# Placing the routing steps of a two-layer transformer kernel earlier and later in its table of steps

## The chip, the core and the metric

The kernel runs on one core of a Trainium2 chip. The metric is the device time of one execution in microseconds (us). A core has five engines, each of which runs its own instructions strictly in order: TensorE (PE, matrix products; its weight loads are listed apart as PEld), VectorE (DVE), ScalarE (ACT), GpSimd (POOL) and SyncE (SP, which here only starts DMA transfers). They wait for each other through semaphores. The before kernel was timed three times: 1833.56, 1834.5 and 1831.23 us, median 1833.56 us.

## What is computed

8192 tokens of width 128 (32 sequences of 256) pass two layers. Layer 0 is a linear attention with 16 heads and rotary positions, beside a mixture of 64 experts of width 64 plus a shared expert. Layer 1 is an attention that keeps the 8 best keys of a row, with a message network over 4 neighbours, followed by a mixture of 8 experts of width 256 of which each token takes 2. Cut to what matters here:

```python
# layer 0, routing: sigmoid scores, 4 of 8 groups, then 8 of 64 experts
scores = sigmoid(x @ router_w.T)
...
coef = zeros((T, E)).at[arange(T)[:, None], topk_idx].add(topk_w)
h = silu(g) * u * coef[:, :, None]
# layer 1, routing: softmax over 8 experts, the best 2
probs = softmax(x @ gate_w.T)
weights, idx = top_k(probs, 2)
weights = weights / sum(weights)
```

Layer 0 computes all 64 experts for every token (the coefficient is zero for the ones not chosen). Layer 1 computes only the two chosen experts of each token: the normalised rows are sent by indirect DMA to slots in HBM that are sorted by expert, and a second phase reads them back block by block.

## The kernel before

Tokens are worked in 16 chunks of 512. In the first phase a chunk is 33 tiles of the layer-0 mixture (32 pairs of experts and the shared expert). One tile is one step `g`; `j` is its number within the chunk, 0 to 32. A step on TensorE is three matmuls into `ps_gate` (L601 to L603), three into `ps_up`, and the down product of three steps earlier into `ps_y` (L656). ScalarE takes `silu` of `ps_gate` (L1260), VectorE multiplies by `ps_up` (L854, `times_up`) and then, a step later, by the coefficients (L848, `times_coef`). The first gate matmul of step g waits for the silu of step g-2, the first up matmul of step g waits for `times_up` of step g-2. So VectorE and ScalarE may be behind by a step and a part, no more.

Everything else (the attention of both layers, the normalisation, the routing of both layers) is cut into small named parts and laid beside those tiles. Tables at the head of the file say at which step `j` a part is put on every engine: `ROUTE0` for the layer-0 routing of the next chunk, `ROUTE1` for the layer-1 routing of the chunk before. An entry of `ROUTE1` at 33 or more falls into the chunk after, at `j` less 33. `make_plan` turns the tables into one list a step, and each engine runs the parts of step `j` that concern it, in the order of the list, behind its tile work:

```python
steps += [(ROUTE1 if c < SPARSE else ROUTE1_LAST, c - 1), (ATTENTION1, c - 1)] if c > 0 else [(PREP1, 0)]
plan[g] += [(what, c - 2) for at, what in ROUTE1 if at == j + TILES0 and c > 1]
plan[g] += [(what, key) for table, key in steps for at, what in table if at == j]
```

The parts of layer-1 routing that carry into the chunk after stand first in the list of their step. They are:

- `rank` (TensorE, L764 and L765): two small products that count the earlier tokens of each expert. It waits for `prefix` on GpSimd.
- `key`, `first2`, `slot` (VectorE; L1065 to L1072, L1076 to L1082, L1085 to L1091): the slot number and the weight of each token. `first2` of a chunk writes `slot_of` (L1082) and waits first until all sends of the chunk before have landed.
- `send0` to `send7` (GpSimd, L1496 to L1503): eight indirect DMAs of 128 rows. Each waits until TensorE has done the gate product of its step; `send0` and `send4` first write two columns of the rows.

The parts of layer-0 routing that the change touches are `sigmoid0` (VectorE: add one, L885, and the reciprocal of one half, L888) and `sigmoid1` (the reciprocal of the other half, L891).

The last chunk of the first phase, number 15, uses the table `ROUTE1_LAST` for chunk 14: `rank` at 17, `first2` at 19, `slot` and `table` (a block table for the second phase, L1171 to L1196) at 20, the sends at 21 to 24. In the same chunk the carried parts of chunk 13 still follow `ROUTE1`. Chunk 0 and chunk 1 have no carried parts.

Three banks of PSUM (`ps_side`) serve all small products in rotation. `make_plan` gives each product a bank when its step is reached and frees it at the step of its reader; TensorE waits for the reader of the bank's last use. Other parts met below: `kv0` to `kv3` (steps 0 to 3: VectorE L971 and L975, then a ScalarE copy L1334), `norm0` (ScalarE L1277, step 2), `q` (TensorE, step 5), `k_rope` (GpSimd L1446, step 4), `q_feat` (GpSimd L1461, step 13), `s0_mask` and `s1_mask` (VectorE L1114, steps 13 and 14), `k_feat` (VectorE L988), `strike0` and `strike1` (VectorE L1129, steps 16 and 17), `attend_exp` (ScalarE L1371, step 18).

Of the kernel before, what the change touches and what calls it, by code (L numbers as in the profile page):

```python
# [70 lines left out]
              (12, "feat_exp"), (13, "q_feat"), (14, "k_feat"), (16, "kvsum"), (17, "kvmask"), (19, "num0"), (20, "num1"), (20, "mix0"),  # L71
              (24, "mix1"), (26, "mixT")]
FINISH0 = [(3, "yT"), (4, "y_add")]
ROUTE0 = [(0, "stats0"), (2, "norm0"), (4, "xT0"), (5, "x_lo0"), (8, "logit0"), (10, "score_exp"), (12, "sigmoid0"), (14, "sigmoid1"),
          (18, "choice"), (18, "pair4"), (19, "pair2"), (20, "pair1"), (21, "gtop"), (22, "gstrike"), (23, "groups"), (24, "top8"),
          (25, "strike"), (26, "weigh"), (28, "coefT")]
ROUTE1 = [(5, "stats1"), (7, "norm1"), (8, "xT1"), (9, "x_lo1"), (10, "vl0"), (10, "vl1"), (11, "top1"), (12, "gate_exp"), (23, "softmax"), (30, "select"),
          (31, "prefix"), (39, "rank"), (40, "key"), (41, "first2"), (42, "slot"), (43, "send0"), (45, "send1"), (47, "send2"), (48, "send3"),
          (49, "send4"), (51, "send5"), (53, "send6"), (54, "send7")]

ROUTE1_LAST = [(5, "stats1"), (7, "norm1"), (8, "xT1"), (9, "x_lo1"), (10, "vl0"), (10, "vl1"), (11, "top1"), (12, "gate_exp"), (14, "softmax"), (15, "select"),
               (16, "prefix"), (17, "rank"), (18, "key"), (19, "first2"), (20, "slot"), (20, "table"), (21, "send0"), (21, "send1"), (22, "send2"), (22, "send3"),
# [25 lines left out]
def make_plan():  # L108
# [11 lines left out]
    for g in range(TILES):  # L120
# [5 lines left out]
        steps += [(ATTENTION0 if c > 0 else EARLY0, c)]  # L126
        steps += [(ROUTE0, c + 1)] if c + 1 < CHUNKS else []
        steps += [(ROUTE1 if c < SPARSE else ROUTE1_LAST, c - 1), (ATTENTION1, c - 1)] if c > 0 else [(PREP1, 0)]
# [1487 lines left out]
```

## Time and profile before

| | us | share of the span |
|---|---|---|
| median of three runs | 1833.56 | |
| the profiled execution's own time | 1833.56 | |
| its span, first to last instruction | 1831.3 | |
| TensorE busy | 1736.6 | 95% |
| VectorE busy | 1348.7 | 74% |
| ScalarE busy | 803.2 | 44% |
| GpSimd busy | 609.8 | 33% |

The span is what the trace shows; 2.3 us of the execution lie outside it. In the chain of work that ended last, 88% is TensorE. Busy time of TensorE is modelled from its pipelined matmuls, so it contains no proof that each matmul ran at its best, but a gap in it is a real gap. The first phase ends near 1509 us of the span, the second phase (the chosen experts of layer 1) takes the rest.

### The profile page before, as it was taken

The numbers are of one execution on the slowest core, as the hardware profiler recorded it, in microseconds if no ns is written. First come the engines' busy times: TensorE is split into PE (matmuls) and PEld (weight loads), VectorE is DVE, ScalarE is ACT, GpSimd is POOL, SyncE is SP. The second block draws the span as 40 slices with busy tenths as digits, with TensorE's granted clock in tenths as the row PEclk, the third lists the DMA queues.
The fourth block names the chain that finished last, engine by engine and source line by source line (L and its number), as shares of the span: only waits on it lengthen the run. The fifth ranks groups of instructions, "written<-read, shape, count | busy, mean of one in ns | idle before, by whom it ended". The sixth has DMA issues, their size and how long they took to land.

```text
span 1831.3 us, 25191 instructions
## 1 busy us (share of the span) xinstructions
PE 1736.6 (95%) x7292; PEld 1225.3 (67%) x7292; DVE 1348.7 (74%) x4012; ACT 803.2 (44%) x1439; POOL 609.8 (33%) x637
## 2 busy tenths in 40 slices
PE   3999999999999999999999999999999989888885
PEld 2667777777777777777767677777777766565653
DVE  5667878787878787878787878787878864553447
ACT  4435353535353535353535353535353434432321
POOL 6212142423232323232323232323231333565550
PEclk9999999999999999999999999999999999999988
DMA  7948464636464636463636363636454444666559
GB/s 213 257 125 238 97 157 101 157 95 163 97 161 97 160 97 160 97 161 94 161 96 163 90 167 94 160 95 162 101 148 102 111 143 141 187 204 213 173 158 298
DMA packets 166470, 269.80 MB, mean 147 GB/s; under 512 B 13688, under 2 KB 52344, under 8 KB 166080
## 3 DMA queue, kind: packets, MB, share of 16 engines
q1 hardware_dynamic: 157760, 250.50, 51.9%
q0 software_dynamic: 8576, 17.70, 3.0%
q8 instruction: 61, 1.00, 0.2%
q14 instruction: 73, 0.60, 0.1%
HBM read 202.21 MB, written 65.93 MB: 146 GB/s over the span
## 4 chain that ended last, share of the span: by engine, by line
PE 88%; another core or an unknown queue 3%; issue 3%; ACT 2%; DMA 2%; DVE 2%; POOL 1%; SPq 0%; ACTq 0%; DVEq 0%; POOLq 0%
PE ps_y L656 24%; PE ps_gate L603 8%; PE ps_gate L602 8%; PE ps_gate L601 7%; PE ps_up L601 7%; PE ps_up L603 7%; PE ps_up L602 7%; PE ps_y L682 3%; PE ps_side L622 2%; PE ps_side L601 2%; PE ps_side L603 2%; PE ps_side L602 2%; PE ps_side L791 1%; PE ps_side L774 1%
## 5 line engine op out<-in xcount | busy, mean ns | idle before, releaser
L854 DVE TENSOR_TENSOR silu_h<-ps_up,silu_h 128x512 f32<-128x512 f32 x618 | 424.4, 687 | 401.9 <-ACT silu_h L1260 260.5
L1260 ACT ACTIVATE silu_h<-ps_gate 128x512 f32<-128x512 f32 x618 | 368.0, 599 | 614.1 <-PE ps_gate L603 535.6
L656 PE MATMUL ps_y<-silu_h,w_dn 128*128 128x512 f32 x1056 | 540.6, 593 | 0.4 <-ACT yT L1266 0.4
L848 DVE TENSOR_TENSOR silu_h<-coef_b,silu_h 128x512 f32<-128x512 f32 x528 | 373.9, 708 | 9.0 <-DMA coef_b<-coef_kept 6.6
L601 PE MATMUL ps_gate<-xnT,w_gu 128*128 128x512 f32 x528 | 318.4, 603 | 0.0
L656 PEld LDWEIGHTS ps_y<-silu_h,w_dn 128*128 128x128 f32 x1056 | 199.4, 189 | 55.0 <-issue 7.7
L601 PE MATMUL ps_up<-xnT,w_gu 128*128 128x512 f32 x528 | 210.3, 398 | 11.0 <-DVE silu_h L854 6.6
L602 PE MATMUL ps_gate<-xnT,w_gu 128*128 128x512 f32 x528 | 211.2, 400 | 0.0
L602 PE MATMUL ps_up<-xnT,w_gu 128*128 128x512 f32 x528 | 209.7, 397 | 0.0
L603 PE MATMUL ps_up<-xnT,w_gu 128*128 128x512 f32 x528 | 209.1, 396 | 0.0
L603 PE MATMUL ps_gate<-xnT,w_gu 128*128 128x512 f32 x528 | 207.4, 393 | 0.0
L1503 POOL DMA_INDIRECT slots_x<-rows,slot_of x120 | 131.4, 1095 | 180.6 <-PE ps_gate L603 153.8
L1482 POOL DMA_INDIRECT y_kept<-ys,y_to x148 | 142.9, 966 | 111.8 <-DVE ys L1221 70.0
L1509 POOL TENSOR_TENSOR msg<-msg 128x512 f32<-128x512 f32 x48 | 72.6, 1513 | 313.4 <-ACT msg L1396 310.9
L601 PEld LDWEIGHTS ps_gate<-xnT,w_gu 128*128 128x128 f32 x528 | 100.1, 190 | 61.1 <-issue 56.8
L602 PEld LDWEIGHTS ps_gate<-xnT,w_gu 128*128 128x128 f32 x528 | 100.1, 190 | 60.0 <-issue 55.5
L601 PEld LDWEIGHTS ps_up<-xnT,w_gu 128*128 128x128 f32 x528 | 99.4, 188 | 39.3 <-DVE silu_h L854 8.0
L682 PE MATMUL ps_y<-silu_h,w_down 128*128 128x512 f32 x180 | 95.9, 617 | 22.8 <-DVE silu_h L854 16.0
L603 PEld LDWEIGHTS ps_up<-xnT,w_gu 128*128 128x128 f32 x528 | 99.7, 189 | 24.5
L603 PEld LDWEIGHTS ps_gate<-xnT,w_gu 128*128 128x128 f32 x528 | 99.0, 187 | 24.0
L602 PEld LDWEIGHTS ps_up<-xnT,w_gu 128*128 128x128 f32 x528 | 99.4, 188 | 22.6
L1441 POOL TENSOR_TENSOR rstd<-rstd,minus_half 128x4 f32<-128x4 f32 x32 | 43.5, 1358 | 174.7 <-DVE shift L866 174.7
(265 smaller groups left out, 2719.9 us busy)
## 6 DMA issues: line engine op xcount, KB each, us to landing
coef_b<-coef_kept SPq DMA_DIRECT2D x256, 512.0 KB
slots_x<-empty SPq DMA_DIRECT2D x15, 2080.0 KB, 12.3
w_block<-w_kept SPq DMA_DIRECT2D x45, 512.0 KB
xs<-slots_x SPq DMA_DIRECT2D x37, 260.0 KB
y_back<-y_kept SPq DMA_DIRECT2D x15, 512.0 KB, 7.1
w_raw<-in_ffn_w SPq DMA_DIRECT2D x49, 128.0 KB, 4.1
w_down<-in_ffn_w SPq DMA_DIRECT2D x45, 128.0 KB
xres<-in_x SPq DMA_DIRECT2D x16, 256.0 KB, 3.1
```

The lines of the kernel that those rows point to most:

```text
L601: eng.matmul(dst, w[0], m[0], start=start, stop=False)
L602: eng.matmul(dst, w[1], m[0], start=False, stop=False)
L603: return eng.matmul(dst, w[0], m[1], start=False, stop=stop)
L656: eng.matmul(ps_y[:, :], w_dn[:, j], silu_h[:, g % HBUFS], start=j == 0, stop=last).then_inc(pe_down)
L682: eng.matmul(ps_y[:, :], w_down[:, t % BUFS1, f], silu_h[:, g % HBUFS], start=first, stop=last).then_inc(pe_down)
L848: eng.tensor_tensor(silu_h[:, s], coef_b[:, q % COEF_RING, k], silu_h[:, s], ALU.mult).then_inc(dve_h)
L854: eng.tensor_tensor(silu_h[:, s], ps_up[g % 2][:, :], silu_h[:, s], ALU.mult).then_inc(dve_h1)
L1260: eng.activation(silu_h[:, s], ps_gate[g % 2][:, :], ACT.Silu).then_inc(act_silu)
L1441: eng.tensor_tensor(rstd[:, layer], rstd[:, layer], minus_half[:, :], ALU.pow).then_inc(pool_rstd[layer])
L1482: eng.indirect_dma_start(y_kept, bass.IndirectOffsetOnAxis(y_to[:, c % XPLACES, r:r + 1], 0), ys[:, c % BUFS1, r], None).then_inc(landed[c ...
L1503: eng.indirect_dma_start(slots_x, bass.IndirectOffsetOnAxis(slot_of[:, r, k:k + 1], 0), rows1[:, c % 2, r], None).then_inc(sent[c % 2], 16)
L1509: eng.tensor_tensor(msg[:, 0], msg[:, 0], msg[:, 1 + k % 2], ALU.add).then_inc(pool_heard)
```

## The change

Two tables of step numbers are altered and nothing else. `sigmoid0` goes from step 12 to 13 and `sigmoid1` from 14 to 16. The carried parts of the layer-1 routing start six steps earlier: `rank`, `key`, `first2`, `slot` from steps 6, 7, 8, 9 of the following chunk to 0, 1, 2, 3, and the eight sends from steps 10 to 21 to steps 4 to 12.

```diff
-ROUTE0 = [... (10, "score_exp"), (12, "sigmoid0"), (14, "sigmoid1"),
+ROUTE0 = [... (10, "score_exp"), (13, "sigmoid0"), (16, "sigmoid1"),
...
-          (31, "prefix"), (39, "rank"), (40, "key"), (41, "first2"), (42, "slot"), (43, "send0"), (45, "send1"), (47, "send2"), (48, "send3"),
-          (49, "send4"), (51, "send5"), (53, "send6"), (54, "send7")]
+          (31, "prefix"), (33, "rank"), (34, "key"), (35, "first2"), (36, "slot"), (37, "send0"), (38, "send1"), (39, "send2"), (40, "send3"),
+          (42, "send4"), (43, "send5"), (44, "send6"), (45, "send7")]
```

`ROUTE1_LAST` is as before, and ScalarE and SyncE have the same instructions in the same order. The three places below are from a chunk in the steady state, that is one of the chunks 2 to 14.

On VectorE, before, step 2 and the start of step 3 (L971 and L975 belong to `kv2`, then `kv3`):

```order
L854 TENSOR_TENSOR silu_h<-ps_up,silu_h 128x512
L971 TENSOR_TENSOR kf<-ps_side,att_const 128x128
L975 TENSOR_TENSOR tmp<-ps_side,att_const 128x16x4 x2
L848 TENSOR_TENSOR silu_h<-coef_b,silu_h 128x512
L854 TENSOR_TENSOR silu_h<-ps_up,silu_h 128x512
L971 TENSOR_TENSOR kf<-ps_side,att_const 128x128
```

and now:

```order
L854 TENSOR_TENSOR silu_h<-ps_up,silu_h 128x512
L1076 MAX gkeys<-gkey 128x8 x4
L1078 RECIPROCAL gsum<-gsum 128x4
L1082 TENSOR_SCALAR slot_of<-gkeys 128x8
L971 TENSOR_TENSOR kf<-ps_side,att_const 128x128
L975 TENSOR_TENSOR tmp<-ps_side,att_const 128x16x4 x2
L848 TENSOR_TENSOR silu_h<-coef_b,silu_h 128x512
L854 TENSOR_TENSOR silu_h<-ps_up,silu_h 128x512
L1085 TENSOR_TENSOR gate<-gate,gsum 128x32
L1086 TENSOR_TENSOR gmatch<-gkey,gkeys 128x64
L1089 TENSOR_TENSOR gmatch<-gmatch,gate 128x64
L1091 TENSOR_REDUCE gw<-gmatch 128x8
```

`first2` and `slot` (and one step earlier `key`) now stand between the tile work and the part that feeds ScalarE's copies of `kv`.

On VectorE, before, steps 12 to 14 (L885 and L888 are `sigmoid0`, L891 is `sigmoid1`, L1114 `s0_mask` and `s1_mask`, L988 `k_feat`):

```order
L885 TENSOR_SCALAR score<-score 128x256
L888 RECIPROCAL score<-score 128x128
L848 TENSOR_TENSOR silu_h<-coef_b,silu_h 128x512
L854 TENSOR_TENSOR silu_h<-ps_up,silu_h 128x512
L1114 SCALAR_TENSOR_TENSOR scores<-ps_side,q_key_bias,causal 128x128
L1114 SCALAR_TENSOR_TENSOR scores<-ps_side,q_key_bias,causal 128x256
L848 TENSOR_TENSOR silu_h<-coef_b,silu_h 128x512
L854 TENSOR_TENSOR silu_h<-ps_up,silu_h 128x512
L988 SCALAR_TENSOR_TENSOR kf<-kf,mix_a 128x512
L891 RECIPROCAL score<-score 128x128
```

and now:

```order
L848 TENSOR_TENSOR silu_h<-coef_b,silu_h 128x512
L854 TENSOR_TENSOR silu_h<-ps_up,silu_h 128x512
L885 TENSOR_SCALAR score<-score 128x256
L888 RECIPROCAL score<-score 128x128
L1114 SCALAR_TENSOR_TENSOR scores<-ps_side,q_key_bias,causal 128x128
L1114 SCALAR_TENSOR_TENSOR scores<-ps_side,q_key_bias,causal 128x256
L848 TENSOR_TENSOR silu_h<-coef_b,silu_h 128x512
L854 TENSOR_TENSOR silu_h<-ps_up,silu_h 128x512
L988 SCALAR_TENSOR_TENSOR kf<-kf,mix_a 128x512
```

`sigmoid0` has moved behind the L854 of step 13 and before `s0_mask`; `sigmoid1` has left step 14 and stands two steps later, before `strike0`.

On GpSimd, before, steps 4 to 10 (L1446 `k_rope`; L1441 and L1443 the layer-1 statistics; L1451, L1455, L1458 parts of the query path; L1496 to L1503 the sends):

```order
L1446 TENSOR_TENSOR kf<-kf,tmp 128x512
L1441 TENSOR_TENSOR rstd<-rstd,minus_half 128x4
L1443 TENSOR_TENSOR shift<-shift,rstd 128x4
L1451 TENSOR_SCALAR mix_a<-kf 128x512
L1455 TENSOR_TENSOR qf<-qf,tmp 128x512
L1458 TENSOR_SCALAR tmp<-qf 128x512
L1496 COPY rows<-gw 128x4
```

and now steps 4 to 8:

```order
L1496 COPY rows<-gw 128x4
L1497 TENSOR_SCALAR rows<-common 128x4
L1503 DMA slots_x<-rows,slot_of 65024x130
L1446 TENSOR_TENSOR kf<-kf,tmp 128x512
L1503 DMA slots_x<-rows,slot_of 65024x130
L1441 TENSOR_TENSOR rstd<-rstd,minus_half 128x4
L1443 TENSOR_TENSOR shift<-shift,rstd 128x4
L1503 DMA slots_x<-rows,slot_of 65024x130
L1451 TENSOR_SCALAR mix_a<-kf 128x512
L1503 DMA slots_x<-rows,slot_of 65024x130
L1455 TENSOR_TENSOR qf<-qf,tmp 128x512
L1458 TENSOR_SCALAR tmp<-qf 128x512
```

The first four sends now stand before and between the attention and statistics parts.

## Rows read from the trace of the kernel before

**Rows 1.** Windows: busy us of each engine, clock, DMA share; chunk 6, chunk 15, a stall.

```profile
core 0: us, PE busy (x) PEld busy (x) DVE busy (x) ACT busy (x) POOL busy (x), PEclk, DMA share, GB/s
583.00:674.80 91.80, 91.80 (x394) 65.29 (x393) 74.03 (x232) 42.96 (x76) 28.11 (x28) 1.00 0.52 129
1409.10:1509.40 100.30, 94.06 (x387) 65.68 (x385) 72.00 (x208) 38.91 (x69) 33.60 (x38) 0.97 0.51 130
1478.00:1484.00 6.00, 4.53 (x10) 3.01 (x11) 5.59 (x16) 0.48 (x1) 3.64 (x3) 0.50 0.17 47
```

**Rows 2.** Timeline, chunk 15: start us, us, engine, line, [idle before <- releaser].

```profile
1471.24 0.17 DVE L1082 TENSOR_SCALAR slot_of<-gkeys 128x8 int32<-128x8 f32 x1 [3.94 <-DMA slots_x<-rows,slot_of]
...
1472.67 0.50 PE L601 MATMUL ps_up<-xnT,w_gu 128*128 128x512 f32 x1 [1.83 <-DVE silu_h L854]
...
1478.73 0.68 DVE L854 TENSOR_TENSOR silu_h<-ps_up,silu_h 128x512 f32<-128x512 f32 x1
...
1479.47 0.80 PE L601 MATMUL ps_up<-xnT,w_gu 128*128 128x512 f32 x1 [4.27 <-issue]
```

**Rows 3.** Timeline of VectorE, chunk 5, steps 7 to 9: the moved parts and what follows.

```profile
514.38 0.18 DVE L1065 TENSOR_TENSOR gkey<-ps_side,left 128x32 f32<-128x32 f32 x1
...
515.10 0.68 DVE L984 TENSOR_TENSOR tmp<-ps_side,att_const 128x512 f32<-128x512 f32 x1
...
516.90 0.36 DVE L1076 MAX8 gkeys<-gkey 128x8 f32<-128x8 f32 x4
...
517.46 0.69 DVE L848 TENSOR_TENSOR silu_h<-coef_b,silu_h 128x512 f32<-128x512 f32 x1
...
520.79 0.18 DVE L1085 TENSOR_TENSOR gate<-gate,gsum 128x32 f32<-128x32 f32 x1
...
521.54 0.68 DVE L882 TENSOR_TENSOR xnT<-ps_side,xnT 128x512 fp32r<-128x512 f32 x1
```

**Rows 4.** Timeline, all engines, chunk 5, steps 2 to 5.

```profile
501.02 0.69 DVE L854 TENSOR_TENSOR silu_h<-ps_up,silu_h 128x512 f32<-128x512 f32 x1 [2.62 <-ACT silu_h L1260]
...
503.92 0.58 ACT L1260 ACTIVATE silu_h<-ps_gate 128x512 f32<-128x512 f32 x1
...
505.67 0.48 PE L601 MATMUL ps_gate<-xnT,w_gu 128*128 128x512 f32 x1
505.72 0.27 ACT L1334 COPY v<-ps_side 128x128 f32<-128x128 f32 x1 [1.22 <-DVE tmp L975]
...
507.61 0.79 PE L601 MATMUL ps_side<-xnT,w 128*128 128x512 f32 x1
```

**Rows 5.** Timeline of VectorE, chunk 5, steps 12 to 14.

```profile
530.74 0.28 DVE L885 TENSOR_SCALAR score<-score 128x256 f32<-128x256 f32 x1
...
531.93 0.63 DVE L848 TENSOR_TENSOR silu_h<-coef_b,silu_h 128x512 f32<-128x512 f32 x1
...
535.24 0.73 DVE L1114 SCALAR_TENSOR_TENSOR scores<-ps_side,q_key_bias,causal 128x128 f32<-128x128 f32 x2
535.89 1.16 DVE L848 TENSOR_TENSOR silu_h<-coef_b,silu_h 128x512 f32<-128x512 f32 x1
536.97 0.68 DVE L854 TENSOR_TENSOR silu_h<-ps_up,silu_h 128x512 f32<-128x512 f32 x1
```

**Rows 6.** Timeline, chunk 5: GpSimd's `q_feat`, and the weight load before TensorE's up product.

```profile
535.20 1.29 POOL L1461 TENSOR_TENSOR qf<-qf,tmp 128x512 f32<-128x512 f32 x1 [5.88 <-ACT qf L1342]
...
538.05 0.19 PEld L601 LDWEIGHTS ps_up<-xnT,w_gu 128*128 128x128 f32 x1
```

**Rows 7.** Timeline, chunk 5, step 28: GpSimd and VectorE starting almost together.

```profile
574.64 1.85 POOL L1509 TENSOR_TENSOR msg<-msg 128x512 f32<-128x512 f32 x1 [2.68 <-ACT msg L1396]
574.66 0.68 DVE L848 TENSOR_TENSOR silu_h<-coef_b,silu_h 128x512 f32<-128x512 f32 x1
```

**Rows 8.** Timeline, ScalarE and TensorE, chunk 5, steps 18 to 21.

```profile
546.50 1.49 ACT L1371 ACTIVATE scores<-scores,top_neg 128x128 f32<-128x128 f32 x4 [0.64 <-DVE rest L1129]
...
549.30 1.09 ACT L1260 ACTIVATE silu_h<-ps_gate 128x512 f32<-128x512 f32 x2
...
550.67 0.49 PE L601 MATMUL ps_gate<-xnT,w_gu 128*128 128x512 f32 x1
```

More of the change, by code:

```diff
@@ L73 @@
 FINISH0 = [(3, "yT"), (4, "y_add")]
-ROUTE0 = [(0, "stats0"), (2, "norm0"), (4, "xT0"), (5, "x_lo0"), (8, "logit0"), (10, "score_exp"), (12, "sigmoid0"), (14, "sigmoid1"),
+ROUTE0 = [(0, "stats0"), (2, "norm0"), (4, "xT0"), (5, "x_lo0"), (8, "logit0"), (10, "score_exp"), (13, "sigmoid0"), (16, "sigmoid1"),
           (18, "choice"), (18, "pair4"), (19, "pair2"), (20, "pair1"), (21, "gtop"), (22, "gstrike"), (23, "groups"), (24, "top8"),
```

## The prediction, made before the changed kernel was run

> **What bounds the kernel now.** I read the busy shares first, then windows of single chunks, then the timeline round the places that the change touches. In a steady chunk TensorE has no gap at all: 91.80 us busy of 91.80, at full clock (1.00, the 2.4 GHz level) [rows 1]. All chunks from 2 to 14 are like that one. So while those chunks last, no part that leaves VectorE or GpSimd gives time back, and TensorE's own work is the same after the change (`rank` costs it the same at step 0 as at step 6). Moving parts can only cost there, where a move makes VectorE or ScalarE later than TensorE's next product. The reader should look for slack, not for busy shares.
>
> Chunk 15 is different: 94.06 us busy in 100.30, clock 0.97 [rows 1]. Its timeline names the cause [rows 2]. VectorE's L1082 (`first2` of chunk 14, step 19) sits 3.94 us until the sends of chunk 13 have landed. These stand at steps 10 to 21, so the wait asks for a send that GpSimd issues only in step 21. Behind L1082 on VectorE stand the products that TensorE needs: it idles 1.83 us and 4.27 us before two up products. The second gap is put down to "issue", but the L854 that ends at 1479.41 releases it 0.06 us later. After it the clock is at 0.50, the 1.2 GHz level, from 1478 to 1484 [rows 1].
>
> **Part 1: the last chunk.** With the sends of chunk 13 at steps 4 to 12, nothing is left for L1082 to wait for. VectorE's work from L1082 to the L854 at 1478.73 is back to back, so TensorE resumes 3.94 us earlier. Its idle time falls from 6.10 to 2.16 us. Next late there is VectorE itself with `table`, which stays. TensorE ran at half clock from 1479.47 to about 1484.5, 5 us that cost 2.5. With a gap of a third of the length this may go wholly (-2.5), half, or not at all; I take the middle, -1.3. Part 1: -5.2, bounds -3.9 and -6.4.
>
> **Part 2: steps 1 to 3 in the steady state.** `key` takes VectorE 515.10 - 514.38 = 0.72 us, `first2` 0.56, `slot` 0.75 [rows 3]. They now stand in front of L971 and L975, for which ScalarE waits with its copy of `kv`, before `norm0` and the next silu. `key` is covered: VectorE sat idle 2.62 us before the L854 of step 2 [rows 4]. From there the 0.56 reach silu at 503.92, which then ends at 504.50 + 0.56 = 505.06; the gate product that needs it starts at 505.67. `first2` and `slot` together, 1.31, reach the copy at 505.72: it ends at 505.99 + 1.31 = 507.30, and `q`, which waits for that PSUM bank, starts at 507.61 [rows 4]. Slack 0.6 and 0.3. Cost taken: 0; if a copy comes 0.5 later than I add up, 0.2 a chunk.
>
> **Part 3: the sends.** Eight indirect DMAs of about 1 us each now stand in GpSimd's queue at steps 4 to 12, in front of `k_rope`, the layer-1 statistics and three query parts. GpSimd is busy 28.11 us of 91.80 [rows 1] and its results are read steps later; the nearest reader is `norm1` at step 7, which feeds products at step 8. SyncE's queue does not change; the sends fall beside SyncE's clearing of the slots at the start of a chunk, with the DMA engines at 0.52 [rows 1]. Cost 0, with up to 0.3 a chunk as the far bound. VectorE loses 0.75 of `slot` in step 9 before a product that TensorE waits for: no gain, as TensorE has no gap there.
>
> **Part 4: `sigmoid0` behind the tile work of step 13.** At step 12 it stood before a long idle stretch of VectorE. It lasts 531.93 - 530.74 = 1.19 us [rows 5]. From step 13 to 18 VectorE is late already and works without a pause. Before, L848 of that stretch took 1.16 us instead of 0.63 to 0.68: it began at 535.89, while GpSimd ran L1461 from 535.20, and ended at 537.05, so it got going at 537.05 - 0.68 = 536.37, which is 1.17 after L1461's start [rows 5, 6]. With 1.19 us of `sigmoid0` in front, L848 starts at 537.08 and is not held any more. The L854 after it moves from 536.97 to 536.97 + 1.19 - 0.48 = 537.68 and ends at 538.36. TensorE needs that end for its up product, whose weight load was at 538.05 [rows 6]. So it waits about 0.3 us, a little less if the masks run quicker (0.73 for a pair that may itself have been held). I take 0.25 a chunk, bounds 0.1 and 0.4. Chunks 1 to 14: 14 x 0.25 = +3.5, bounds +1.4 and +5.6.
>
> **Part 5: `sigmoid1` at step 16.** The reciprocal of half the scores takes at most 1.19 - 0.28 = 0.91. It leaves step 14, so VectorE has caught up there, and comes back before `strike0`. At `strike1` VectorE is 0.71 later than before. ScalarE's exponentials waited for that 0.64 us already; they start at 547.2 in place of 546.50, the silu pair at 550.0 in place of 549.30, and its first half ends at 550.6, with the gate product at 550.67 + 0.25 [rows 8]. That just fits. 0.04 a chunk: +0.5, bounds 0 and +2.
>
> **Sum.** The profiled execution took 1833.56 us (span 1831.3 and 2.3 outside it) and is the median of the three. 1833.56 - 5.2 + 3.5 + 0.5 = 1832.4; rounded, 1832. The second phase moves forward as a block.
>
> **The rivals.** 0.2%, or 3.7 us, is what a measurement of this kernel can tell from no change.
>
> GpSimd gets in first at step 13 (slower). L885 would start at 535.24, and GpSimd's L1461 starts at 535.20, in all these chunks 0.03 to 0.04 earlier. If L885 is held as L848 was, it waits until 536.37, 1.13 more. L854 then ends at 538.36 + 1.13 = 539.49 and TensorE loses 1.4 a chunk in place of 0.25: 14 x 1.4 = 19.6, and 1833.56 - 5.2 + 19.6 = 1848. It decides from the point where GpSimd's start counts before VectorE's. Against it: at step 28 L1509 started 0.02 before an L848 and it was L1509 that was held (1.85 against 1.29 for L1461), L848 took its usual 0.68 [rows 6, 7]. For it: the lead is double that.
> The Trainium skill (SBUF — State Buffer, "Who interferes with whom") says that VectorE and GpSimd share one pair of SBUF ports as an exclusive lock, that a `tensor_scalar` in its two-port mode takes it, and that the instruction that issues first blocks the other for its whole length. By that rule and the start times, this rival is the forecast, 1848; the step-28 rows show that the earlier recorded start is not always the one that gets the lock.
>
> No stall at step 13 or 21 (faster). If the masks and L848 run 0.3 quicker than I add up, only part 1 is left: 1833.56 - 5.2 = 1828.4. For it: the L1114 pair was beside L1461 and may shrink. Against: two parts have to be off in the same direction.
>
> The carried parts overrun the slack of steps 2 to 6 (slower). The slack of `q` is 0.3, and VectorE's later L848 now meets `k_rope`, which also comes later; if it is held there as in rows 5 and ScalarE runs 0.8 late, TensorE loses 0.5 a chunk: 1832.4 + 7 = 1839.4.
>
> The change doesn't give what it can in chunk 15: `slot`, `table` or a port wait fills the 3.94. Then 1833.56 + 4.0 = 1837.6. Against it: nothing between L1082 and L854 waits for another engine.
>
> **How the numbers follow.** Forecast 0.48, own range 1828.5 to 1836.5; GpSimd first 0.15; no stall 0.20; overrun 0.12; nothing in chunk 15 0.05. Range for 8 in 10: 1827 to 1842, which leaves out the case of 1848 and a little below. Faster than 1829.9: most of the no-stall case and a tenth of the forecast, 0.25. Slower than 1837.2: GpSimd first, most of the overrun, half of the last case and a few hundredths of the forecast, 0.24. Same 0.51.
>
> **What would show it.** In the windows chunk 15 should take some 95 us, and L1082 there should have no wait. The 1.83 gap should be gone, the 4.27 gap be near 2.2, and the low clock shorter. A steady chunk should be 92.0 to 92.2 us long, with one short wait of the up product of step 16 for L854; a chunk of 93 us with L885 lasting over 1 us is the first rival, one of 91.8 is the no-stall case, and a wait before `q` or the gate product of step 5 is the overrun. I am wrong altogether if chunk 15 stays at 100 us, or if the second phase changes its length by more than some 3 us.

## The result: slower, and the profile after

The changed kernel takes 1852.45 us (median of 6, 1847.48 to 1858.4) against 1833.19 before; the ratio is 1.0099 (95%: 1.0075 to 1.0124), a loss of 19 us where 1832 and no change were forecast. Its profiled execution took 1840.88 us (span 1838.6). That is below all six timed ones: its second phase happened to be 11 us shorter than before's (below), so the comparison here goes by chunks and by the start of the second phase. A chunk is counted from its first gate product to the next chunk's.

| | before | after | difference |
|---|---|---|---|
| chunk 1 | 92.68 us | 95.48 us | +2.80 |
| a chunk from 3 to 14 | 91.79 us | 93.52 us | +1.73 |
| chunk 15 | 100.24 us | 93.81 us | -6.43 |
| start of the second phase | 1509.34 us | 1528.12 us | +18.78 |

The windows of the changed kernel, chunk 6 and chunk 15, answer to [rows 1]; the columns are the same:

```profile
core 0: us, PE busy (x) PEld busy (x) DVE busy (x) ACT busy (x) POOL busy (x), PEclk, DMA share, GB/s
592.60:686.10 93.50, 92.39 (x394) 65.02 (x393) 77.20 (x232) 43.11 (x76) 25.42 (x28) 1.00 0.49 126
1434.30:1528.10 93.80, 91.33 (x386) 64.21 (x385) 73.40 (x208) 38.94 (x69) 33.48 (x38) 1.00 0.50 129
```

TensorE had no gap in chunk 6 and now has 1.1 us of them, both before an up product that waits for L854: 1.00 at step 16 and 0.11 at step 8. VectorE is busy 3.2 us longer with the same 232 instructions. Of that 1.1 belong to L885 and 2.4 to the 32 L848 together. Instructions that last longer with the same work may have been held, so the next view is the timeline of VectorE, GpSimd and the up products at steps 12 to 16 of chunk 6. It answers to [rows 5, 6]:

```profile
636.35 0.69 DVE L854 TENSOR_TENSOR silu_h<-ps_up,silu_h 128x512 f32<-128x512 f32 x1 [3.08 <-PE ps_up L603]
636.92 1.29 POOL L1461 TENSOR_TENSOR qf<-qf,tmp 128x512 f32<-128x512 f32 x1 [2.65 <-ACT qf L1342]
636.95 1.41 DVE L885 TENSOR_SCALAR score<-score 128x256 f32<-128x256 f32 x1
...
638.40 0.95 DVE L888 RECIPROCAL score<-score 128x128 f32<-128x128 f32 x1
639.27 0.64 DVE L1114 SCALAR_TENSOR_TENSOR scores<-ps_side,q_key_bias,causal 128x128 f32<-128x128 f32 x2
639.83 0.68 DVE L848 TENSOR_TENSOR silu_h<-coef_b,silu_h 128x512 f32<-128x512 f32 x1
640.42 0.68 DVE L854 TENSOR_TENSOR silu_h<-ps_up,silu_h 128x512 f32<-128x512 f32 x1
...
641.16 0.51 PE L601 MATMUL ps_up<-xnT,w_gu 128*128 128x512 f32 x1 [1.00 <-DVE silu_h L854]
```

L885, `sigmoid0`'s addition, takes 1.41 us; [rows 5] had it at 0.28. It starts 0.03 after GpSimd's L1461 and is done 1.44 after it, of which 0.28 is its own work: it got going some 1.16 after L1461's start, as L848 did before [rows 5, 6]. Everything behind it on VectorE is 1.13 later, and the up product of step 16 waits. By steps, the chunk loses 1.3 us at step 16 and 0.4 at step 8. The second loss begins at step 5:

```profile
609.76 1.12 POOL L1503 DMA_INDIRECT slots_x<-rows,slot_of  x1 [0.88 <-POOL rows L1497]
...
610.82 1.95 DVE L848 TENSOR_TENSOR silu_h<-coef_b,silu_h 128x512 f32<-128x512 f32 x1
610.92 1.29 POOL L1446 TENSOR_TENSOR kf<-kf,tmp 128x512 f32<-128x512 f32 x1
...
612.70 0.68 DVE L854 TENSOR_TENSOR silu_h<-ps_up,silu_h 128x512 f32<-128x512 f32 x1
```

L1446 is `k_rope`, now queued behind the first early send. L848 lasts 1.95 instead of 0.68 although its recorded start is 0.10 earlier; less its own 0.68 it got going 1.17 after L1446's start. In the kernel before, L1446 started 0.16 behind an L848 in all these chunks, that L848 took 0.68 and L1446 1.66 to 1.68.

A third meeting changed sides as well. At step 28 of the kernel before, GpSimd's L1509 was the one held (1.85 us, [rows 7]). In the changed kernel its first instruction of the pair is unheld (1.28 us) and an L848 that comes 0.46 later is held. No step of the chunk there is longer than before.

```profile
677.73 2.97 POOL L1509 TENSOR_TENSOR msg<-msg 128x512 f32<-128x512 f32 x2 [2.25 <-ACT msg L1396]
678.19 1.37 DVE L848 TENSOR_TENSOR silu_h<-coef_b,silu_h 128x512 f32<-128x512 f32 x1
```

In chunk 15 the wait of L1082 is gone, which answers to [rows 2]; of two gaps of TensorE one is left, and the clock is at 1.00 throughout:

```profile
1492.18 0.17 DVE L1082 TENSOR_SCALAR slot_of<-gkeys 128x8 int32<-128x8 f32 x1
...
1500.41 0.50 PE L601 MATMUL ps_up<-xnT,w_gu 128*128 128x512 f32 x1 [2.47 <-issue]
```

### The profile page after: what moved, and what is told of

The parts are those of the page before. It is cut to its first block, busy times and chain, and to the rows that moved or that the text cites. A ratio compares the mean times of both kernels' runs of the same rounds, so it can differ in the third digit from the quotient of the medians.

```text
span 1838.6 us, 25191 instructions
## 1 busy us (share of the span) xinstructions
PE 1735.0 (94%) x7292; PEld 1215.0 (66%) x7292; DVE 1395.8 (76%) x4012; ACT 806.5 (44%) x1439; POOL 580.0 (32%) x637
## 4 chain that ended last, share of the span: by engine, by line
PE 76%; DVE 10%; issue 5%; ACT 4%; another core or an unknown queue 2%; DMA 2%; POOL 1%; SPq 0%; DVEq 0%; ACTq 0%; POOLq 0%
PE ps_y L656 20%; PE ps_up L601 7%; PE ps_up L603 6%; PE ps_up L602 6%; PE ps_gate L602 6%; PE ps_gate L603 6%; PE ps_gate L601 6%; PE ps_y L682 3%; DVE silu_h L854 3%; DVE silu_h L848 2%; PE ps_side L622 2%; PE ps_side L601 2%; ACT silu_h L1260 2%; PE ps_side L603 2%
## 5 line engine op out<-in xcount | busy, mean ns | idle before, releaser
L854 DVE TENSOR_TENSOR silu_h<-ps_up,silu_h 128x512 f32<-128x512 f32 x618 | 424.2, 686 | 363.4 <-ACT silu_h L1260 210.2
L848 DVE TENSOR_TENSOR silu_h<-coef_b,silu_h 128x512 f32<-128x512 f32 x528 | 405.6, 768 | 10.6 <-DMA coef_b<-coef_kept 7.2
L1509 POOL TENSOR_TENSOR msg<-msg 128x512 f32<-128x512 f32 x48 | 65.2, 1357 | 543.0 <-ACT msg L1396 541.0
L1503 POOL DMA_INDIRECT slots_x<-rows,slot_of x120 | 137.2, 1143 | 49.8 <-issue 22.3
L602 PEld LDWEIGHTS ps_up<-xnT,w_gu 128*128 128x128 f32 x528 | 99.5, 188 | 20.7
L1441 POOL TENSOR_TENSOR rstd<-rstd,minus_half 128x4 f32<-128x4 f32 x32 | 43.8, 1368 | 142.0 <-DVE shift L866 142.0
```

The lines of the kernel that those rows point to most:

```text
L602: eng.matmul(dst, w[1], m[0], start=False, stop=False)
L848: eng.tensor_tensor(silu_h[:, s], coef_b[:, q % COEF_RING, k], silu_h[:, s], ALU.mult).then_inc(dve_h)
L854: eng.tensor_tensor(silu_h[:, s], ps_up[g % 2][:, :], silu_h[:, s], ALU.mult).then_inc(dve_h1)
L1441: eng.tensor_tensor(rstd[:, layer], rstd[:, layer], minus_half[:, :], ALU.pow).then_inc(pool_rstd[layer])
L1503: eng.indirect_dma_start(slots_x, bass.IndirectOffsetOnAxis(slot_of[:, r, k:k + 1], 0), rows1[:, c % 2, r], None).then_inc(sent[c % 2], 16)
L1509: eng.tensor_tensor(msg[:, 0], msg[:, 0], msg[:, 1 + k % 2], ALU.add).then_inc(pool_heard)
```

## The experiments

The theory: three effects that add up. The early tail takes 6.4 us out of chunk 15; `sigmoid0` at step 13 loses a tie for the SBUF port shared by VectorE and GpSimd, 1.35 us a chunk; the early sends move `k_rope` into a second tie, 0.37 a chunk. The lines of `ROUTE1` that carry over, from `rank` to the sends, are called the tail here, and a meeting of two instructions whose starts lie close together is called a tie. Ratios are against runs of the kernel before on the same chip; they differ from the quotient of the two medians by up to 0.001. That kernel's median was 1832.53 us beside the first four kernels, 1788.79 beside the next four and 1791.50 beside the last four; the unchanged steady chunk takes 91.79 us in the profiles of all three sessions, so only ratios and chunks are compared.

| kernel | a chunk from 4 to 13 | chunk 15 | ratio, 95% interval |
|---|---|---|---|
| before | 91.79 | 100.24 | |
| after | 93.52 | 93.81 | 1.0099, 1.0075 to 1.0124 |
| tail_only | 92.15 | 93.84 | 0.9988, 0.9974 to 1.0001 |
| sig_only | 93.14 | 99.69 | 1.0081, 1.0063 to 1.0099 |
| sig1_only | 91.79 | 100.49 | one run |
| sig_qfeat14 | 92.02 | 100.69 | one run |
| mask_first | 92.51 | 100.09 | one run |
| nudge | 92.02 | 94.79 | 0.9985, 0.9971 to 1.0000 |
| nudge_in_place | 92.39 | 95.28 | 1.0002, 0.9991 to 1.0012 |
| send_after_rope | 91.79 | 95.27 | 0.9981, 0.9969 to 0.9993 |
| last_only | 91.79 | 95.23 | 0.9974, 0.9956 to 0.9992 |
| last_table | 91.79 | 93.19 | 0.9973, 0.9959 to 0.9987 |
| pad | 90.98 | 98.96 | 0.9922, 0.9905 to 0.9938 |
| last_table_pad | 90.98 | 95.37 | 0.9909, 0.9892 to 0.9925 |

### The two halves apart: tail_only, sig_only, sig1_only

tail_only is the kernel before with the changed `ROUTE1`; sig_only is it with the changed `ROUTE0`; sig1_only moves `sigmoid1` alone.

```diff
 # sig1_only
-(12, "sigmoid0"), (14, "sigmoid1"),
+(12, "sigmoid0"), (16, "sigmoid1"),
```

(The first expectation calls L885 a compare and L1461 a multiply-reduce; L885 is the addition of one, L1461 an addition.)

> Only the routing tail is early, as in the changed kernel; both sigmoids stand at steps 12 and 14, as before. Theory (two ties for the port that VectorE and GpSimd share, one at step 13 by sigmoid0 beside the routing sum of GpSimd, worth 1.3 us a chunk, and one at step 5 to 8 by k_rope behind the early routing step, worth 0.4; the early tail takes 6.4 out of chunk 15): the compare by capacity on VectorE (L885) starts before GpSimd's multiply-reduce L1461 and takes 0.28 us, the stall before step 16 is gone, a steady chunk takes 92.1 to 92.2 us, chunk 15 about 93.8, the second phase starts within 2 us of the kernel before, and the ratio is about 1.000. Rival (the early tail and its two sends are the whole loss, the sigmoids harmless): a steady chunk of 93.5, ratio 1.010.

> Only the sigmoids are moved, to steps 13 and 16; the routing tail is where it was. Theory: L885 stands one sigmoid (some 0.3 to 0.7 us) later, falls behind the start of GpSimd's L1461 and is held about 1.1 us; the stall before step 16 is there, a steady chunk takes about 93.1 us, chunk 15 is still about 100.2, and the second phase starts about 18 us later; ratio 1.010. Rival (the tail is the loss): a steady chunk of 91.8 and ratio 1.000.

> The kernel before with sigmoid1 alone moved, 14 to 16. Theory (all of the sigmoids' loss is sigmoid0's add of one, L885, beside L1461): a steady chunk takes 91.8 us, L891 simply stands later. Rival (the second reciprocal adds to the load at step 16 and is part of the stall): a steady chunk of 92.2 or more.

The chunks of all three went by the theory. The ratio of sig_only came out at 1.0081 where 1.010 was expected, and its second phase started 20.7 us later instead of 18. The halves add up: 0.36 + 1.35 = 1.71 a chunk, 1.73 together. In tail_only L885 is back at 0.28 us (626.55) while L848 is held behind `k_rope`. `sigmoid1` costs nothing. So `sigmoid0` is what made the kernel slower. The tail costs 0.36 a chunk too, but gives it back in chunk 15.

### Is it the port? sig_qfeat14, mask_first

Both leave VectorE's work as it is in sig_only and shift the meeting of L885 and L1461. sig_qfeat14 runs GpSimd's part one step later; mask_first puts L885 behind the first masking in the same step.

```diff
 # sig_qfeat14
-(12, "feat_exp"), (13, "q_feat"),
+(12, "feat_exp"), (14, "q_feat"),
 # mask_first
+        plan[g].sort(key=lambda step: step[0] == "sigmoid0")
```

> The sigmoids at 13 and 16 and nothing else of the change, and GpSimd's step q_feat (with its multiply L1461) one step later, at 14, so that it isn't beside L885. Theory (the port): L885 takes 0.28 us again, the stall before step 16 falls from 1.3 us to 0.3 or less, and a steady chunk takes 91.8 to 92.2 us, unless L1461 now meets another VectorE step. Rival (VectorE simply has more to do in step 13 than it has room for): the stall stays about 1.3 us and the steady chunk about 93.1.

> Sigmoids at 13 and 16 and the routing tail as before, but within step 13 sigmoid0 stands behind the first masking of the attention scores (L1114, with a source in PSUM), so that L885 starts some 0.65 us later against L1461. Theory (the hold ends at a fixed time, about 1.17 us after L1461's start): L885 lasts about 0.5 us instead of 1.40, the stall before step 16 is 0.9 us shorter or more, and a steady chunk takes 92.0 to 92.3 us. Rival (a VectorE instruction that meets L1461 is delayed by a fixed amount whenever it comes): L885 still 1.4 us, steady chunk 93.1.

In sig_qfeat14 L885 starts 0.45 before L1461 and takes 0.28 us, and the chunk 92.02: of the 1.35 us 1.12 are gone, with the same VectorE instructions in the same order. The rival "VectorE has too much to do in step 13" falls; its share is at most the 0.23 that is left, of which 0.15 stands at step 16 and the rest at steps 19 and 23. In mask_first, the timeline of chunk 6 (VectorE and GpSimd):

```profile
631.19 1.30 POOL L1462 TENSOR_TENSOR qf<-qf,tmp 128x512 f32<-128x512 f32 x1 [5.88 <-ACT qf L1343]
631.23 0.73 DVE L1115 SCALAR_TENSOR_TENSOR scores<-ps_side,q_key_bias,causal 128x128 f32<-128x128 f32 x2
631.88 0.76 DVE L886 TENSOR_SCALAR score<-score 128x256 f32<-128x256 f32 x1
```

(Line numbers are one higher.) L886 starts 0.69 after L1462 and ends 1.45 after it: again 1.17 plus 0.28. The hold runs to a fixed time after GpSimd's start, and the later one comes the less is left of it; the rival (1.4 us whenever it comes) falls. I had expected "about 0.5 us" and 92.0 to 92.3: I had left the instruction's own 0.28 out; 92.51 follows with it, since L886 ends where L885 ended in sig_only and only the 0.64 of masking is already done (93.14 - 0.64 = 92.50). The masking, which has a source in PSUM, went on beside L1462: 0.73 us for the pair, against 0.64 in the changed kernel, where L1461 is over.

### Who gets the port: nudge, nudge_in_place

Both are the changed kernel with one more GpSimd instruction, so that L1461 comes a few hundredths later. They differ in where it writes.

```diff
                     eng.wait_ge(act_qrelu, c + 1)
+                    eng.memset(nudge, 0.0)
                     eng.tensor_tensor(qf[:, :], qf[:, :], tmp0[:, :], ALU.add)
 # nudge: a new buffer of one element, ahead of y_to
 # nudge_in_place: a spare element behind wsum0, no address changes
```

> The changed kernel with one more instruction on GpSimd in every q_feat: a memset of one element per partition into a buffer that nothing reads, between its wait and its multiply-add L1461, so that L1461 starts some 0.05 to 0.15 us later. Theory (who holds the shared port is decided by a few hundredths of a us at step 13): L885 now takes the port first and lasts 0.28 us instead of 1.41, L1461 waits for it, the stall before step 16 falls by 1.0 to 1.3 us, a steady chunk takes 92.2 to 92.5 us instead of 93.5, and the ratio to the kernel before falls from 1.010 to 1.001 to 1.003: 0.1 us more work on GpSimd makes the kernel 15 us or more faster. Rival (the stall is the amount of VectorE work in steps 13 to 16): a steady chunk of 93.5 and a ratio of 1.010.

> The changed kernel with the same added memset on GpSimd as in the run before it, but into a spare element of an existing buffer, so that no buffer's address changes. Theory (in the run before, two things happened: L885 took the port first, and, since the new buffer had moved the weights by 32 bytes, each matmul took 391 ns instead of 396): matmuls take 396 ns, L885 0.28 us, the stall before step 16 is 0.3 us or less, a steady chunk takes 92.5 to 92.8 us, and the ratio is 1.003 to 1.006. Rival (the memset alone did both): 391 ns, a steady chunk of 92.0, ratio 0.9985.

The timeline of nudge_in_place, chunk 6:

```profile
632.48 0.10 POOL L1462 MEMSET small<- 128x1 f32 x1 [1.52 <-ACT qf L1343]
632.54 1.44 POOL L1463 TENSOR_TENSOR qf<-qf,tmp 128x512 f32<-128x512 f32 x1
632.54 0.28 DVE L886 TENSOR_SCALAR score<-score 128x256 f32<-128x256 f32 x1
```

Now both start in the same hundredth, VectorE has the port, L886 takes 0.28 and GpSimd's instruction is the longer one (1.44 against 1.29). So it is in all 14 chunks, as in the changed kernel L885 was held in all 14. An instruction added to GpSimd makes a chunk 1.13 us shorter, 16 us in 14 chunks, and takes the ratio from 1.0099 to 1.0002. From end to end of their intervals the ratios are 0.6 to 1.3% apart, 11 to 24 us. This is the cause shown both ways. I had expected a ratio of 1.003 to 1.006 and 92.5 to 92.8 us; the chunk is 0.1 better than that. The ratio is 0.003 better, which the chunks don't explain: in its profile the second phase still starts 5.6 us later than in the kernel before (1514.96 against 1509.34).

The run nudge was to show the same, and its 0.9985 was too good: its chunk of 92.02 is 0.37 shorter than that of nudge_in_place, and even its steps without any routing work took 2.24 us in place of 2.26. The new buffer had moved the weights.

### The second tie: send_after_rope

```diff
-(36, "slot"), (37, "send0"), (38, "send1"), (39, "send2"), (40, "send3"),
-(42, "send4"), (43, "send5"), (44, "send6"), (45, "send7")]
+(36, "slot"), (38, "send0"), (39, "send1"), (40, "send2"), (41, "send3"),
+(43, "send4"), (44, "send5"), (45, "send6"), (46, "send7")]
```

> The early routing tail of the changed kernel in all chunks, sigmoids as before, but every send one step later, so that GpSimd's k_rope (L1446) at step 4 isn't behind the first send. Theory (the 0.37 us a chunk of the early tail is the multiply L848 held by L1446 behind the send): a steady chunk takes 91.8 to 91.9 us, chunk 15 about 93.8 to 95.2, ratio 0.9965 to 0.998. Rival (the 0.37 us are from the early rank at steps 0 to 3, or from the sends as such): a steady chunk stays at 92.1 to 92.2, ratio about 0.999 to 1.000.

It went by the theory: 91.79. The rank parts are still early, the sends only a step later, and in the timeline `k_rope` is the held one, as it was in the kernel before:

```profile
601.34 0.68 DVE L848 TENSOR_TENSOR silu_h<-coef_b,silu_h 128x512 f32<-128x512 f32 x1
601.50 1.67 POOL L1446 TENSOR_TENSOR kf<-kf,tmp 128x512 f32<-128x512 f32 x1 [9.13 <-DVE tmp L975]
```

### The version that beats both: last_only, last_table

last_only is the kernel before with the early tail in chunk 15 alone, where it pays.

```diff
-plan[g] += [(what, c - 2) for at, what in ROUTE1 if at == j + TILES0 and c > 1]
+plan[g] += [(what, c - 2) for at, what in (ROUTE1 if c < SPARSE else ROUTE1_EARLY) if at == j + TILES0 and c > 1]
```

> The kernel before with the early routing tail in the last chunk alone (its order of routing work differs from that of the other chunks only there). Theory (the early tail empties the end of chunk 15, which has no next chunk to carry the late tail, and costs nothing else): steady chunks 91.8, chunk 15 93.8 instead of 100.2, second phase 6.4 us earlier, ratio 0.9965. Rival (the second phase absorbs it, since it waits for something of its own such as weights or the gathers): chunk 15 93.8, second phase longer by 6, ratio 1.000. Rival (the tail of chunk 15 was short in the changed kernel only because its sigmoids were late too): chunk 15 over 96, ratio above 0.998.

Faster than both: ratio 0.9974 (medians 1828.9 and 1832.53 us). By the ratio that is 4.8 us (1.5 to 8.1) where 6.4 were expected; send_after_rope, at 0.9981, can't be told from it. The first rival (the second phase absorbs the gain, ratio 1.000) falls. Chunk 15 of the profiled run took 95.23, not 93.8. The difference is the clock, in a window of chunk 15 behind the gap that is left:

```profile
1478.00:1482.00 4.00, 4.00 (x14) 3.11 (x13) 2.40 (x7) 1.57 (x3) 2.06 (x4) 0.63 0.10 33
```

After the same idle time of TensorE, 2.47 us, the granted clock stayed at 1.00 in tail_only and in the changed kernel, and fell here to its 1.2 GHz level for some 3 us. The five profiles with the early tail, an uncut table and the weights where they were gave a chunk 15 of 93.81 (after), 93.84, 95.23, 95.27 and 95.28: the granted clock of the chunk is 1.00 in the first two and 0.98 in the other three. So -6.4 is the good end, -5 came three times. Why the same gap has two outcomes is open.

last_table also cuts the row of small VectorE instructions in front of that gap into four pieces.

```diff
-(20, "slot"), (20, "table"), (21, "send0"),
+(20, "slot"), (21, "send0"),
+(23, "table0"), (24, "table1"), (25, "table2"), (26, "table3")]
```

> The early routing tail in the last chunk alone, as tried, and there the table of blocks for the second phase (13 small VectorE instructions, 4 us in a row at step 20) cut into four pieces at steps 23 to 26. Theory (in chunk 15 that row keeps the multiplies L848 and L854 waiting, and TensorE idles 2.5 us before step 21): that idle time is gone, chunk 15 takes 91.5 to 93 us instead of 93.8 to 95.2, ratio 0.995 to 0.997. Rival (the pieces delay the same multiplies two steps later, or the second phase's first loads wait for the table): chunk 15 as long as before the cut, ratio 0.9974.

The gap that the row at step 20 caused is gone (TensorE's step 23 takes 3.7 us instead of 7.7), but the ratio is the same, 0.9973, outside the 0.995 to 0.997 that I expected. About half of the gain in chunk 15 is taken back in step 28, which is 2.3 us longer: TensorE now waits for the second phase's first rows. Chunk 15 is 2.0 us shorter than in last_only, 93.19 against 95.23, which is less than these ratios can tell.

```profile
1494.82 0.63 PE L804 MATMUL ps_side<-common,xs 128*128 128x128 f32 x4 [2.08 <-DMA xs<-slots_x]
```

### The address of the weights: pad, last_table_pad

```diff
+        pad = sb("pad", [1])
         y_to = sb("y_to", [XPLACES, ROWS], INT32)
```

> The kernel before with one more buffer of one element, which nothing uses, ahead of y_to: all buffers behind it, the weights w_gu and w_dn among them, lie 32 bytes higher. Theory (the address of the weights sets the matmul's pace): the matmuls of 512 columns take 391 ns instead of 396, a step without routing work 2.235 us instead of 2.265, a steady chunk about 91.2 us, and the ratio is about 0.994 or lower if the second phase gains too. Rival (the address does nothing): 396 ns, 91.8 us, ratio 1.000.

> Both of the last two: early tail in the last chunk alone, the table in four pieces, and the weights 32 bytes higher. Theory (the three add up): a steady chunk of 91.2 us, chunk 15 under 93, ratio 0.989 to 0.992. Rival (the address does nothing): 91.8 us, ratio 0.996.

An unused buffer of four bytes makes the kernel before 0.8% faster, ratio 0.9922. The second product of each three, 300 to 1400 us (busy us, mean ns), before and then pad, where line numbers are one higher:

```profile
L602 PE MATMUL ps_gate<-xnT,w_gu 128*128 128x512 f32 x396 | 158.4, 400 | 0.0
L602 PE MATMUL ps_up<-xnT,w_gu 128*128 128x512 f32 x395 | 156.5, 396 | 0.0
```

```profile
L603 PE MATMUL ps_gate<-xnT,w_gu 128*128 128x512 f32 x400 | 156.3, 391 | 0.0
L603 PE MATMUL ps_up<-xnT,w_gu 128*128 128x512 f32 x399 | 155.9, 391 | 0.0
```

The six gate and up forms sum to 2579 ns before and 2557 with the pad, most of it in these two. The starts show the same. In the five steps of a chunk that hold no small product (15, 18, 22, 30, 31; chunks 3 to 13) a step takes 2.262 us before and 2.235 with the pad. Of these 27 ns, 15 lie between the second gate product and the third (240 to 226) and 9 between the second up product and the third (236 to 227). No other interval changes by more than 4, and the down product not at all, although `w_dn` has moved too. So I had it wrong that all matmuls go from 396 to 391 ns: it is two of the six. 33 steps of 27 ns would make 0.89 us; a chunk is 0.81 shorter.

By the buffer sizes in the kernel, `xnT` lies where it was, and `w_gu` and `w_dn`, which began 32 bytes past a multiple of 64 from the first buffer, now begin on one; every other buffer from `y_to` on has moved as well. That the alignment, and not another effect of the shift, is the cause was not tried. With last_table it is the fastest kernel of this study, 0.9909; the two gains add up only in part, because chunk 15 (95.37, where under 93 was expected) waits longer in step 28 for the same rows.

## Why the prediction was wrong

**Bounds.** Right: no gap in a steady chunk, so every lost tie counts in full, and only chunk 15 has something to give.

**Part 1 (last chunk), -5.2, bounds -3.9 and -6.4.** Right in mechanism; -6.43 in the changed kernel's profile, where the low clock went away wholly, about -5.0 in three of the five profiles. The gap that is left is 2.47 us, not 2.16, and another 0.38 came from step 17, which I had not looked at.

**Part 2 (steps 1 to 3), 0.** Right. Step 0 takes 0.45 longer and step 6 0.45 less, which is `rank`'s own work moved, and `q` comes without a gap.

**Part 3 (sends), 0, far bound 0.3.** Wrong in size: 0.36 to 0.38 a chunk, 5 us in all. I looked at who reads the late results of GpSimd and not at what its late instructions would meet on the port. The rival "overrun" named the meeting of L848 and `k_rope` and priced it 0.5, but hung it on the slack of `q`.

**Part 4 (sigmoid0), 0.25 a chunk.** This is the step that failed, in the sentence "L848 starts at 537.08 and is not held any more". It is true of L848, but it took for granted that the instruction in L848's place, L885, would be first at the port. The size that the step worked out was right for that case: 0.23 where the meeting is avoided (sig_qfeat14), 92.39 - 92.15 = 0.24 where VectorE wins it (nudge_in_place). In part that is luck: only 0.15 of it stands at step 16, where I had put all of it. VectorE didn't win it: 1.35 a chunk, as the first rival had priced (1.4, 1848 us, given 0.15), a case that the range of 1827 to 1842 left out. I gave it so little on one pair of rows, [rows 7], where GpSimd's recorded start was 0.02 earlier and GpSimd still lost. The trace of the kernel before has ten such pairs of L1509 and L848, with GpSimd ahead by 0.01 to 0.03, and it lost them all; it has none with the 0.04 of L885. So these rows spoke for leads up to 0.03 and said nothing on 0.04. The 14 chunks all have the same lead, so they are one toss, not fourteen, and the chance was on the whole 15 us.

The Trainium skill (SBUF — State Buffer, "Who interferes with whom") gave the right side by the recorded starts of step 13, and the wrong one for `k_rope`, where VectorE's recorded start was first by 0.10 and GpSimd had the port. That page of the Trainium skill has the holder keep the pair for its whole instruction; by the rows VectorE got going 1.17 us after the start of GpSimd's 1.29, a little before its recorded end.

**Part 5 (sigmoid1), +0.5.** Nothing was measured (sig1_only, 91.79), the lower of its bounds.

**Second phase "as a block".** It started 18.8 us later and the median is 19.3 later, so in the median, yes. A single profile doesn't show it: its length was 322.0 before and 310.5 after. A change of 3 us, which I had named as a sign of being wrong altogether, was no sign of anything.

Sum by what was measured: -6.4 + 13 x 1.73 + 2.8 in chunk 1 = +18.9. How much of chunk 1's 2.8 is the change's isn't shown: that chunk took 96.13 us in last_table, where it has the order of the kernel before, against 92.68.

## What to carry to other kernels

When a VectorE instruction that can be held by GpSimd is moved, write down the distance between its new start and the nearest GpSimd instruction that reads SBUF, and price both outcomes if it is small; here VectorE lost with starts from 0.28 earlier to 0.04 later. A constant lead in a periodic schedule decides for the whole run. Where the outcome isn't sure, move one of the two by a step: that was free here (send_after_rope put `k_rope` back at its old 0.16 behind L848), and it gives the early tail without its cost. Apply a remedy where its bottleneck is: the early tail paid in one chunk of sixteen.

## What the runs showed of the hardware

- The hold of a VectorE instruction by GpSimd's 128x512 `tensor_tensor` of 1.29 us ends 1.14 to 1.19 us after that one's start, whenever the VectorE instruction arrives (L848 from 0.28 earlier to 0.88 later, L885 at +0.03, L886 at +0.69). Where the GpSimd instruction is recorded with 1.55 or 1.58 us, it ends at 1.41 to 1.45 (L848 beside L1509 and L1455). GpSimd's 128x512 `tensor_scalar` (L1451, L1458, chunk 6 of the changed kernel) held L848 only until some 0.5 after its start.
- The recorded starts don't decide alone. GpSimd won with a lead of 0.03 to 0.04 (L1461 before L885, 28 chunks of two kernels), lost with 0.01 to 0.03 (L1509, ten chunks of the kernel before), and lost in the same hundredth (nudge_in_place). L1446, close behind an indirect DMA, won 0.10 after VectorE in most chunks of the changed kernel and 0.28 after it in chunk 2; not behind one, it lost at 0.16 (before and send_after_rope). A line at a lead of about 0.03 would divide all these cases but those of L1446. Why L1446 won is open. The indirect DMA by itself didn't hold such an L848: in chunk 6 of sig_only one that started inside a 1.07 us indirect DMA took 0.68.
- Four unused bytes ahead of the weights: two of the six gate and up products of a step come 15 and 9 ns sooner, 0.8% of the kernel.
- The length of the second phase goes by the occasion, not by the kernel: 310.5 to 322.0 us in the profiles of before, after and the first four experiments, 274.6 to 278.1 in those of the last eight. The kernel before itself had medians of 1832.53, 1788.79 and 1791.50 us in the three sessions. Waits of the silu there (us in total, times, longest), before and then sig1_only:

```profile
ACT silu_h L1260 <- remote: 56.9, 12, 6.8
```

```profile
ACT silu_h L1260 <- PE ps_gate L603: 85.3, 48, 3.2
```

In the kernel before ScalarE waits 12 times, up to 6.8 us, for something that the profile calls remote; in sig1_only no such wait is among the longest. What it is stays open.
